# Two heads side by side in the rows of TensorE, in units of 512 columns, and the causal cut of P moved to GpSimd

## The chip, the cores and the metric

One core of one Trainium2 chip runs the whole program in one launch. The metric is the device time in microseconds (us); before the change three runs gave a median of 1901.57 us (1899.66 to 1901.57).

## The reference

The input x has 2 batches of 1024 tokens of width 128. Three layers follow each other; the first and the third are the same function (here called the FFN layer):

```python
q, k, v = to_heads(split(x @ w_qkv, 3))                      # 16 heads of width 8
scores = einsum('bhqd,bhkd->bhqk', q, k) / sqrt(8)
attn = softmax(where(causal, scores, -big))
o = einsum('bhqk,bhkd->bhqd', attn, v) -> (b, s, 128) @ w_o
h = layernorm(x + o); then a mixture of 8 experts (top 2, hidden width 512), layernorm
x = x + 0.5 * that
```

The middle layer is another attention, with selected keys. The change touches only the causal attention of 16 heads in the first and the third layer.

## The kernel before, in words

Every engine runs one hand-written instruction stream, and semaphores order them. One FFN layer is: layer norm (DVE), transposes and the products with w_qkv (PE), then the attention, then the output product, the gate and the 8 experts.

Attention goes in steps. A step is a pair of heads (`s` = 0, 1) of one batch; there are `PAIRS` = 16 steps per layer and 32 in the program. Since a head has only 8 dimensions, q and k are split into three bf16 parts each, and all nine products are stacked in the contraction: 72 rows (`ROWS`) of `QB[buf][s]` and `KB[buf][s]`, which SyncE's queue fills from DRAM (`sp_rows`, 12 loads of 24 rows and one of V a step; a ring of 4 buffers). The parts are made by a ping-pong between ScalarE (`p1_done`, `p2_done`) and VectorE (`r1_done`, `p3_done`) and spilled to DRAM first.

A step has two passes over the lower triangle of the 1024 x 1024 scores, each in 24 units of one head, one tile and at most 512 columns:

- Pass 1 (`pe_pass1`): scores with queries in partitions. PE adds the causal mask of a diagonal block with a product of the identity and `mask_qk`; VectorE takes the row maximum from PSUM (`dve_max`, line 1299). It runs one step ahead. `dve_maxrows` makes three bf16 parts of minus the maximum, PE transposes them (`pe_maxrows`, line 658), and ScalarE copies them as rows 96 to 98 into `QB` (`act_maxrows`, line 1065).
- Pass 2 (`pe_scores`): scores with keys in partitions, less the maximum (99 rows), again with a mask product (`mask_kq`, line 673). ScalarE takes the exponential from PSUM into `PT` (`act_exps`, line 1059).
- `pe_values` (line 687) multiplies V (32 columns: 8 of V, a 1 for the row sum, zeros) by P in float32. A float32 product is two passes over the array. Its output for head s and query half hf lies in strip (2s + hf) of 32 partitions of bank 6, so four strips can run side by side. It is called once for each key tile `kc`.
- ScalarE copies the result (line 1077), PE transposes it (line 696), VectorE divides by the sums and writes `ATT` (line 1328).

PSUM has three banks for pass 1, three for pass 2, one for the values, one for transposes. `pe_step` interleaves one unit of pass 2 with one of pass 1.

Of the kernel before, what the change touches and what calls it, by code (L numbers as in the profile page):

```python
# [16 lines left out]
P = 128  # L17
# [117 lines left out]
PT_RING = 8  # L135
# [12 lines left out]
def constants():  # L148

    f = np.float32  # L150
    q, k = np.arange(P)[:, None], np.arange(P)[None, :]
    sel = LW + np.arange(NSEL)[None, :]
    override = sel > q

    sign = np.where(np.arange(P) % DR < HALF, -1.0, 1.0)[:, None]
    c = {"ident": np.eye(P),
         "mask_qk": np.where(k > q, NEG, 0.0),
         "mask_kq": np.where(q > k, NEG, 0.0),
         "iota8": np.broadcast_to(np.arange(E), (P, E)),
         "nonlocal": np.where(k <= q, 3e38, -3e38),  # L160
         "keep": np.where(override, 0.0, 1.0),
         "fill": np.where(override, np.broadcast_to(sel, (P, NSEL)), 0.0),
         "key": np.arange(P)[:, None] + P * np.arange(4)[None, :],
         "swap": np.eye(P)[np.arange(P) ^ HALF],
         "sign": sign}
    return {n: np.ascontiguousarray(v.astype(f)) for n, v in c.items()}
# [33 lines left out]
def build(nc, ins, const_ap, rot_ap, mask_ap, out):  # L200
# [3 lines left out]
    q_rows = nc.dram_tensor("q_rows", (PAIRS, 2, HD, 3, L), BF16, kind="Internal").ap()  # L204
    k_rows = nc.dram_tensor("k_rows", (PAIRS, 2, HD, 3, L), BF16, kind="Internal").ap()
# [4 lines left out]
    with ExitStack() as ctx:  # L210
# [6 lines left out]
        bank = [ctx.enter_context(nc.psum_tensor(f"bank{i}", [P, BANK], F32)) for i in range(8)]  # L217
# [9 lines left out]
        mask_qk = sb("mask_qk_b", [P, P], BF16)  # L227
        mask_kq = sb("mask_kq_b", [P, P], BF16)
# [67 lines left out]
        qparts = view("ffn", (3, TOK), BF16)  # L296
        kparts = view("ffn", (3, TOK), BF16)
# [8 lines left out]
        rest = view("ffn", (2, BANK))  # L306
        VA = view("ffn", (PAIRS, 2, TB, STRIP))
        QB = [[view("ffn", (L,), BF16) for h in range(2)] for i in range(RING)]
        KB = [[view("ffn", (L,), BF16) for h in range(2)] for i in range(RING)]
        VS = [view("ffn", (2, TB, STRIP)) for i in range(RING)]  # L310
        OT = view("ffn", (BANK,))
        PT = [view("ffn", (BANK,)) for i in range(PT_RING)]
        rowmax = view("ffn", (2, 2, TB))
# [63 lines left out]
        qk_done, p1_done, r1_done, p2_done, p3_done = (sem(n) for n in ("qk_done", "p1_done", "r1_done", "p2_done", "p3_done"))  # L377
# [39 lines left out]
        EXP0, PV0, ATT0, GELU0, Y0, ACC0, MAX0, OTURN0, OT0 = S_RING, 2 * TB, 2, 4, 2, 2, S_RING, 1, 1  # L417
# [5 lines left out]
        def sp_rows(sp, c, it, buf):  # L423

            g = PAIRS * c
            if not isinstance(it, int) or c:
                sp.wait_ge(pv_done, PV0 + TB * (g + it - RING + 1))
            for s in range(2):
                for dst, src, axis in ((QB, q_rows, 1), (KB, k_rows, 0)):

                    rows = src[it:it + 1, s] if isinstance(it, int) else src[bass.ds(it, 1), s]
                    rows = rows.rearrange("a d r t -> r (a d) t").unsqueeze(axis).broadcast_to([3, 3, HD, L])
                    for i in range(3):
                        sp.dma_start(dst[buf][s][i * 3 * HD:(i + 1) * 3 * HD, :], rows[i]).then_inc(rows_loaded[buf], 16)
# [20 lines left out]
        def sp_ffn(sp, c):  # L455
# [118 lines left out]
        def pool_ffn(pool, c):  # L574
# [5 lines left out]
            pool_fill(pool, c)  # L580
            for n in (ln + 1, ln + 2):
                pool_rstd(pool, n)

        def pool_fill(pool, c):
# [5 lines left out]
            pool.memset(MB[:, :, :], 0.0)  # L590
            for buf in range(RING):
                for s in range(2):
                    pool.drain()
                    pool.memset(QB[buf][s][64:MAXROW, :], 0.0)
                    pool.memset(KB[buf][s][64:MAXROW, :], 0.0)
                    pool.drain()
                    pool.memset(KB[buf][s][MAXROW:MAXROW + MAXROWS, :], 1.0)
                pool.drain()
                pool.memset(spare[:, 3:4], float(c)).then_inc(filled, 1)

# [35 lines left out]
        def pe_pass1(pe, c, it, buf, u, visit):  # L636

            s, qt, hf = UNITS1[u]
# [3 lines left out]

            pe.wait_ge(max_done, MAX0 + N1 * n + u + 1 - S_RING)
            lo, hi = hf * BANK, min((qt + 1) * P, (hf + 1) * BANK)
            o = bank[u % S_RING]
            m = pe.matmul(o[:, 0:hi - lo], QB[buf][s][0:ROWS, qt * P:(qt + 1) * P], KB[buf][s][0:ROWS, lo:hi], start=True, stop=True)  # L646
            if hi == (qt + 1) * P:
                m = pe.matmul(o[:, hi - lo - P:hi - lo], ident_b[:, :], mask_qk[:, :], start=False, stop=True, skip_group_check=True)  # L648
            m.then_inc(s1_done, 1)

        def pe_maxrows(pe, c, it):
# [5 lines left out]
            for qt in range(TB):  # L657
                m = pe.transpose(mt[:, qt * P:(qt + 1) * P], MB[:, qt, :], ident_b[:, :])
            m.then_inc(mt_done, 1)

        def pe_scores(pe, c, it, buf, w):

            s, kc, hf = UNITS2[w]
            n = PAIRS * c + it
            if w == 0:
                pe.wait_ge(maxrow_ready, 2 * n + 2)

            pe.wait_ge(exp_done, EXP0 + N2 * n + w + 1 - S_RING)
            lo, hi = max(kc * P, hf * BANK), (hf + 1) * BANK
            o, rows = bank[S_RING + w % S_RING], MAXROW + MAXROWS  # L670
            m = pe.matmul(o[:, 0:hi - lo], KB[buf][s][0:rows, kc * P:(kc + 1) * P], QB[buf][s][0:rows, lo:hi], start=True, stop=True)  # L671
            if lo == kc * P:
                m = pe.matmul(o[:, 0:P], ident_b[:, :], mask_kq[:, :], start=False, stop=True, skip_group_check=True)  # L673
            m.then_inc(st_done, 1)

        def pe_values(pe, c, it, buf, kc):

            units = [w for w in range(N2) if UNITS2[w][1] == kc]
            n = PAIRS * c + it
            if kc == 0:  # L680
                pe.wait_ge(ot_ready, OT0 + n)
            pe.wait_ge(exp_done, EXP0 + N2 * n + units[-1] + 1)
            for w in units:
                s, _, hf = UNITS2[w]
                lo = max(kc * P, hf * BANK)
                r = (2 * s + hf) * STRIP
                m = pe.matmul(bank[6][r:r + STRIP, lo - hf * BANK:BANK], VS[buf][:, s, kc, :],  # L687
                              PT[w % PT_RING][:, 0:(hf + 1) * BANK - lo], start=(kc == 0), stop=True, skip_group_check=True)
# [10 lines left out]
        def ahead_units(left):  # L699

            return [(1, u) for u in range(EARLY, N1) if left >= 1] + [(2, u) for u in range(EARLY) if left >= 2]

        def pe_step(pe, c, b, it, buf, left, visit):

            todo = ahead_units(left)

            def ahead(n):
                for _ in range(min(n, len(todo))):
                    a, u = todo.pop(0)
                    pe_pass1(pe, c, it + a, (buf + a) % RING, u, visit + (buf + a) // RING)  # L710

            for kc in range(1, TB + 1):
                for w in [w for w in range(N2) if UNITS2[w][1] == kc]:
                    pe_scores(pe, c, it, buf, w)
                    ahead(1)
                if kc == MAX_AT and left >= 1:
                    pe_maxrows(pe, c, it + 1)
                pe_values(pe, c, it, buf, kc - 1)
            if left >= 1:
                pe_first_scores(pe, c, it + 1, (buf + 1) % RING, ahead)  # L720
            pe_outputs(pe, c, it)

        def pe_first_scores(pe, c, it, buf, ahead):
            for w in [w for w in range(N2) if UNITS2[w][1] == 0]:
                pe_scores(pe, c, it, buf, w)
                ahead(1)

        def pe_ffn(pe, c):
# [3 lines left out]
            for n in range(8):  # L732
                if n % 2 == 0:
                    pe.wait_ge(xt_ready, NG * n_turn + n // 2 + 1)
                if n >= 4:
                    pe.wait_ge(r1_done, 8 * c + n - 3)
                pe.matmul(bank[4 + n % 4][:, :], w_qkv[:, (n % 2) * D:(n % 2 + 1) * D],
                          XT[:, (n // 2) * BANK:(n // 2 + 1) * BANK], start=True, stop=True).then_inc(qk_done, 1)
# [7 lines left out]
            pe.wait_ge(r1_done, 8 * (c + 1))  # L746
            for u in range(N1):
                pe_pass1(pe, c, 0, 0, u, 0)
            pe_maxrows(pe, c, 0)
            todo = list(range(EARLY))  # L750

            def ahead(n):
                for _ in range(n * EARLY // 4):
                    pe_pass1(pe, c, 1, 1, todo.pop(0), 0)

            pe_first_scores(pe, c, 0, 0, ahead)
# [1050 lines left out]
```

## Time and profile before

| | |
|---|---|
| median of 3 runs | 1901.57 us |
| the profiled execution's own time | 1901.23 us |
| its span, first to last instruction | 1899.4 us |
| PE busy / VectorE / ScalarE / GpSimd | 86% / 69% / 58% / 18% |
| granted clock of TensorE, mean | 0.885 of 2.4 GHz |

### The profile page before, as it was taken

What the parts mean: (1) busy time and instruction counts of PE and PEld (TensorE: products, weight loads), DVE (VectorE), ACT (ScalarE), POOL (GpSimd) and SP (SyncE); (2) the same over time, 40 slices, a digit from 0 to 9 for tenths busy, and PEclk for the clock granted to TensorE, in tenths of its full rate; (3) what the DMA queues carried; (4) which work ended last, traced back from release to release, by engine and by line L of the source; (5) the groups of instructions that cost most, each with busy time, mean ns of one, the idle gap of its engine ahead of it and who ended that gap; (6) DMA issues with size and microseconds to landing.
All of it is one profiled execution on the core that took longest, in us unless ns stands there. A gap on an engine that the chain in (4) does not pass through costs nothing.

```text
span 1899.4 us, 34045 instructions
## 1 busy us (share of the span) xinstructions
PE 1626.6 (86%) x10724; PEld 954.2 (50%) x10724; DVE 1316.8 (69%) x3191; ACT 1110.8 (58%) x2328; POOL 336.6 (18%) x343
## 2 busy tenths in 40 slices
PE   3699999879995836599999999984799999879995
PEld 2244444357774412355555555663344444357774
DVE  5577777467778565777768787645677777557777
ACT  3276777558884534345446445542377677558873
POOL 6000000000001050154446444615000000000000
PEclk9599999969998755798689998996699999969998
DMA  4211111011110223411122121202111110011110
GB/s 139 72 43 49 46 47 35 1 57 67 66 56 16 81 67 83 92 56 32 52 65 72 36 57 55 77 24 94 68 48 45 53 44 31 1 57 67 66 56 23
DMA packets 67657, 104.28 MB, mean 55 GB/s; under 512 B 19560, under 2 KB 37424, under 8 KB 65456
## 3 DMA queue, kind: packets, MB, share of 16 engines
q1 hardware_dynamic: 57872, 84.87, 14.2%
q0 software_dynamic: 8192, 16.79, 3.3%
q8 instruction: 73, 1.20, 0.3%
q10 hardware_dynamic: 1456, 0.90, 0.2%
q14 instruction: 64, 0.52, 0.1%
HBM read 74.80 MB, written 8.59 MB: 44 GB/s over the span
## 4 chain that ended last, share of the span: by engine, by line
PE 71%; DVE 12%; ACT 5%; issue 4%; DVEq 4%; SPq 2%; DMA 1%; ACTq 0%; POOL 0%; POOLq 0%
PE bank L687 11%; PE bank L833 9%; PE bank L671 8%; PE bank L646 7%; PE bank L823 6%; PE bank L987 5%; PE bank L1000 2%; PE bank L1015 2%; PE bank L1003 2%; DVEq L1624 2%; PE bank L1031 2%; PE bank L968 2%; ACT experts L1132 2%; PE bank L648 2%; PE bank L673 2%
## 5 line engine op out<-in xcount | busy, mean ns | idle before, releaser
L1299 DVE TENSOR_REDUCE arena<-bank 128x1 f32<-128x512 f32 (+3 forms) x768 | 382.8, 551 | 168.9 <-PE bank L648 115.7
L1059 ACT ACTIVATE arena<-bank 128x512 f32<-128x512 f32 (+3 forms) x768 | 335.3, 493 | 143.8 <-PE bank L673 121.2
L624 POOL DMA_INDIRECT arena<-kv_rows,IDX x256 | 251.8, 984 | 368.3 <-PE bank L1034 244.1
L646 PE MATMUL bank<-arena 72*128 72x512 bf16 (+3 forms) x768 | 259.5, 346 | 38.9 <-DMA arena<-arena 36.9
L671 PE MATMUL bank<-arena 99*128 99x512 bf16 (+3 forms) x768 | 254.2, 335 | 6.1 <-ACT arena L1065 4.3
L572 POOL TENSOR_TENSOR rstd<-vareps,neghalf 128x8 f32<-128x8 f32 x14 | 23.2, 1659 | 1170.8 <-DVE vareps L1292 1170.8
L687 PE MATMUL bank<-arena 128*32 128x512 f32 (+3 forms) x1536 | 225.4, 501 | 0.0
L1357 DVE TENSOR_TENSOR experts<-arena,experts 128x512 fp32r<-128x512 f32 x256 | 171.5, 689 | 70.7 <-ACT experts L1132 70.7
L1130 ACT ACTIVATE arena<-bank,bias 128x512 f32<-128x512 f32 x256 | 185.9, 726 | 45.8 <-PE bank L823 45.8
L823 PE MATMUL bank<-experts,experts 128*128 128x512 f32 x768 | 196.7, 403 | 7.5 <-ACT experts L1132 5.4
L1132 ACT ACTIVATE experts<-bank,bias 128x512 fp32r<-128x512 f32 x256 | 187.2, 731 | 0.0
L833 PE MATMUL bank<-experts,experts 128*128 128x512 f32 x768 | 182.1, 389 | 0.0
L671 PEld LDWEIGHTS bank<-arena 99*128 99x128 bf16 x768 | 75.3, 98 | 204.1 <-ACT arena L1059 139.9
L823 PEld LDWEIGHTS bank<-experts,experts 128*128 128x128 f32 x768 | 143.6, 192 | 54.7 <-ACT experts L1132 22.3
L833 PEld LDWEIGHTS bank<-experts,experts 128*128 128x128 f32 x768 | 144.2, 188 | 30.4
L1264 ACT ACTIVATE ATT<-bank,col 128x256 f32<-128x256 f32 x128 | 60.7, 474 | 133.9 <-DVE col L1697 132.1
L1688 DVE TENSOR_TENSOR HN<-bank,RT 96x512 f32<-96x512 f32 x128 | 87.0, 680 | 71.2 <-PE bank L987 59.6
L646 PEld LDWEIGHTS bank<-arena 72*128 72x128 bf16 x768 | 77.8, 101 | 109.8 <-DVE arena L1299 44.5
L648 PE MATMUL bank<-mask_qk_b,ident_b 128*128 128x128 bf16 x512 | 117.2, 230 | 0.0
L673 PE MATMUL bank<-mask_kq_b,ident_b 128*128 128x128 bf16 x512 | 113.0, 222 | 0.0
L987 PE MATMUL bank<-XN,arena 128*96 128x512 bf16 x408 | 111.7, 416 | 0.2 <-DVE HN L1688 0.2
L1270 ACT ACTIVATE ATT<-ATT,inverse 128x256 f32<-128x256 f32 x128 | 64.6, 505 | 74.6 <-DVE inverse L1702 74.4
(249 smaller groups left out, 2436.4 us busy)
## 6 DMA issues: line engine op xcount, KB each, us to landing
arena<-wt_rows SPq DMA_DIRECT2D x16, 1024.0 KB, 4.9
arena<-q_rows SPq DMA_DIRECT2D x192, 48.0 KB
arena<-k_rows SPq DMA_DIRECT2D x192, 48.0 KB
arena<-in_L_ffn_w SPq DMA_DIRECT2D x32, 256.0 KB, 5.3
arena<-arena SPq DMA_DIRECT2D x32, 256.0 KB
XT<-idx_rows SPq DMA_DIRECT2D x16, 512.0 KB
arena<-kv_rows,IDX POOLq DMA_INDIRECT x256
arena<-HN SPq DMA_DIRECT2D x32, 128.0 KB, 2.4
```

Of the source, the lines that this page charges most:

```text
L624: pool.indirect_dma_start(G[d % GR][:, g, :], None, kv_rows, bass.IndirectOffsetOnAxis(ap=IDX[:, q, k * GB + g:k * GB + g + 1], axis=0))\
L646: m = pe.matmul(o[:, 0:hi - lo], QB[buf][s][0:ROWS, qt * P:(qt + 1) * P], KB[buf][s][0:ROWS, lo:hi], start=True, stop=True)
L671: m = pe.matmul(o[:, 0:hi - lo], KB[buf][s][0:rows, kc * P:(kc + 1) * P], QB[buf][s][0:rows, lo:hi], start=True, stop=True)
L687: m = pe.matmul(bank[6][r:r + STRIP, lo - hf * BANK:BANK], VS[buf][:, s, kc, :], PT[w % PT_RING][:, 0:(hf + 1) * BANK - lo], start=(kc == ...
L823: m = pe.matmul(bank[f][:, :], W1R[buf][w][:, f * P:(f + 1) * P], XR[x][:, tb * BANK:(tb + 1) * BANK], start=((w, x) == pairs[0]), stop=(( ...
L833: m = pe.matmul(bank[4 + k][:, :], W2R[buf][w][:, f, :], H1R[k][x][:, f, :], start=(f == 0 and (w, x) == pairs[0]), stop=(f == FC - 1 and ...
L987: m = pe.matmul(o[0:ROWKV, :], TAB[part][:, 4 * b + c, 0:ROWKV], OH[OH_AT[x][c] % OHR][:, :], start=(c == 0 and part == 0), stop=(c == n - ...
L1059: act.activation(PT[w % PT_RING][:, 0:m], bank[S_RING + w % S_RING][:, 0:m], ACT.Exp, scale=float(HD) ** -0.5)\
L1130: act.activation(H1[tb % 2][:, f, :], bank[f][:, :], ACT.Gelu_apprx_tanh, bias=bias1[buf][:, f:f + 1])
L1132: act.activation(H1R[tb % 2][0][:, f, :], bank[f][:, :], ACT.Gelu_apprx_tanh, bias=bias1[buf][:, f:f + 1]).then_inc(gelu_done, 1)
L1299: dve.tensor_reduce(rowmax[:, hf, s, qt:qt + 1], bank[u % S_RING][:, 0:n], AX_X, ALU.max).then_inc(max_done, 1)
L1357: dve.tensor_tensor(H1R[tb % 2][1][:, f, :], H1[tb % 2][:, f, :], H1R[tb % 2][0][:, f, :].bitcast(F32), ALU.subtract)\
```

## The change

- Two parts of float32r in place of three of bf16, so 4 products of 8 rows: 32 rows, and 3 rows for the maximum, which are zero in pass 1 (`zero_rows`, loaded by DMA) and hold the maximum in pass 2. `ROWS` is 35. Both heads of a step share one `QB[buf]` and one `KB[buf]`: head 0 in partitions 0 to 34, head 1 in 64 to 98 (`TILE` = 64), that is in two row halves of TensorE.
- A unit is now both heads by 512 columns: 9 units (`UNITS`) in place of 24 in each pass. Segments of several tiles are packed into one unit (`PASS1`, `PASS2`). It fills two PSUM banks, a `twin`, and one VectorE or ScalarE instruction reads all 1024 columns.
- The query tiles are ordered `QORDER` = 0,3,4,7 and 1,2,5,6, so that both strips of a head have the same number of blocks. Values run in 5 groups of units (`GROUPS`).
- Both passes share three twins (`S_RING` = 3) in turn. Pass 1 runs two steps ahead. Pass 2 has no mask product; GpSimd sets the upper triangle of P to zero in `PT` (`pool_cut`), and the values wait for that (`cut_done`). Pass 1 keeps its masks only in the last two units (4 diagonal blocks each, one 512-column product a head).
- The split of q and k is one ScalarE copy and one VectorE subtraction per 512 columns.
- Ahead of the first pass 1 of each layer PE runs 64 bf16 products of 128x128 by 512 columns into bank 7, whose result is not used.

The core of the diff:

```diff
-UNITS1 = [(s, t, hf) for t in range(TB) for s in range(2) for hf in range(2) if hf * BANK < (t + 1) * P]
-UNITS2 = [(s, kc, hf) for kc in range(TB) for hf in range(2) for s in range(2) if (hf + 1) * BANK > kc * P]
+PASS1 = [[(4, 0, 4)], [(5, 0, 4)], [(6, 0, 4)], [(7, 0, 4)], [(3, 0, 3), (1, 0, 1)], [(7, 4, 3), (5, 4, 1)], [(2, 0, 2), (6, 4, 2)],
+         [(t, t, 1) for t in MORDER[:4]], [(t, t, 1) for t in MORDER[4:]]]
+PASS2 = [[(0, 0)], [(1, 0)], [(1, 1)], [(0, 1), (0, 7)], [(0, 2), (0, 5)], [(1, 2), (1, 6)], [(0, 3), (0, 6)], [(1, 3), (1, 5)],
+         [(0, 4), (1, 4)]]
+GROUPS = [(0, 1), (2, 3), (4, 5), (6, 7), (8,)]
...
+        def pool_cut(pool, c, it, buf, u):
...
+            pool.wait_ge(exp_done, done)
+            p = PT[(UNITS * buf + u) % PT_RING]
+            for at in diagonals(u):
+                cut = p[:, :, at * P:(at + 1) * P]
+                m = pool.affine_select(out=cut, in_=cut, pattern=[[0, 2], [1, P]], compare_op=ALU.is_ge, fill=0.0, base=0, channel_multiplier=-1)
+            m.then_inc(cut_done, 1)
...
+            for j, (qt, k0, blocks) in enumerate(PASS1[u]):
+                for s in range(2):
+                    r = slice(TILE * s, TILE * s + ROWS)
+                    q = QPLACE[qt]
+                    m = pe.matmul(bank[2 * slot + s][:, at * P:(at + blocks) * P], QB[buf][r, q * P:(q + 1) * P],
+                                  KB[buf][r, k0 * P:(k0 + blocks) * P], start=(j == 0), stop=True, skip_group_check=True)
...
+        def pe_scores(pe, c, it, buf, u, left):
+            if left >= 2:
+                pe.wait_ge(max_done, MAX0 + TOTAL * c + m + UNITS + EARLY - 1)
...
+        def pe_next(pe, c, it, buf, m, u, visit):
+            pe.wait_ge(exp_done, EXP0 + TOTAL * c + m)
+            pe_pass1(pe, c, it, buf, u, visit, (2 * ((u + HALFWAY) % UNITS) + 1) % S_RING)
...
+            two, one = (buf + 2) % RING, (buf + 1) % RING
+            for u in range(HALFWAY, UNITS):
+                pe_scores(pe, c, it, buf, u, left)
+                if left >= 2:
+                    pe_next(pe, c, it + 2, two, UNITS * it + u, u - HALFWAY, visit + (buf + 2) // RING)
+                if u == HALFWAY:
+                    pe_values(pe, c, it, buf, 1)
+                if u == HALFWAY + 1 and left >= 1:
+                    pe_maxrows(pe, c, it + 1)
+                if u == HALFWAY + 2:
+                    pe_values(pe, c, it, buf, 2)
...
+            for u in range(HALFWAY):
+                pe_scores(pe, c, it + 1, one, u, left)
+                if left >= 2:
+                    pe_next(pe, c, it + 2, two, UNITS * (it + 1) + u, u + EARLY, visit + (buf + 2) // RING)
+                if u == 0:
+                    pe_values(pe, c, it, buf, 3)
+                if u == 1:
+                    pe_values(pe, c, it, buf, 4)
+                if u == 3:
+                    pe_values(pe, c, it + 1, one, 0)
+            pe_outputs(pe, c, it)
+
+        def pe_warm(pe):
+            for _ in range(WARM):
+                pe.matmul(bank[7][:, :], ident_b[:, :], mask_qk[:, :, :].rearrange("p a q -> p (a q)"), start=True, stop=True)
...
+            pe_warm(pe)
+            for x in range(UNITS + EARLY):
+                pe.wait_ge(max_done, MAX0 + TOTAL * c + x - S_RING + 1)
+                pe_pass1(pe, c, x // UNITS, x // UNITS, x % UNITS, 0, (2 * x + 2) % S_RING)
```

## Rows read from the trace of the kernel before

**Rows 1.** The page: busy time of each engine, and the granted clock in 40 slices.
```profile
PE 1626.6 (86%) x10724; PEld 954.2 (50%) x10724; DVE 1316.8 (69%) x3191; ACT 1110.8 (58%) x2328; POOL 336.6 (18%) x343
...
PEclk9599999969998755798689998996699999969998
```

**Rows 2.** Busy time by stretches: stretch, length, PE, PEld, DVE, ACT, POOL, clock, DMA.
```profile
42.50:87.00 44.50, 25.03 (x104) 10.51 (x105) 20.74 (x47) 7.36 (x12) 4.23 (x6) 0.50 0.30 106
87.00:368.00 281.00, 277.75 (x2138) 122.48 (x2136) 192.91 (x483) 200.80 (x420) 0.00 (x0) 1.00 0.11 37
...
700.00:840.00 140.00, 97.55 (x487) 47.22 (x486) 88.26 (x171) 61.01 (x118) 30.61 (x31) 0.73 0.34 79
840.00:1000.00 160.00, 154.15 (x1208) 93.72 (x1205) 113.20 (x289) 75.55 (x213) 72.38 (x76) 0.81 0.18 51
1000.00:1200.00 200.00, 190.99 (x1673) 117.44 (x1674) 160.20 (x410) 107.70 (x301) 103.40 (x106) 0.94 0.20 55
```

**Rows 3.** The chain that ended last, 250 to 300 us: start, length, what.
```profile
257.84 0.45 PE bank L658 x8
...
264.36 0.44 PE bank L696 x4
...
275.85 0.45 PE bank L658 x8
```

**Rows 4.** Groups by line and shape, 120 to 330 us: count, busy, mean ns, idle before.
```profile
L1299 DVE TENSOR_REDUCE arena<-bank 128x1 f32<-128x512 f32 x140 | 91.9, 685 | 26.5 <-PE bank L646 19.1 <-PE bank L648 7.4
...
L1065 ACT ACTIVATE arena<-bank 3x1024 bf16<-3x1024 bf16 x22 | 22.3, 1013 | 1.7
...
L1299 DVE TENSOR_REDUCE arena<-bank 128x1 f32<-128x128 f32 x46 | 12.0, 282 | 0.0
```

**Rows 5.** PE's timeline, 196 to 199 us.
```profile
196.73 0.22 PE L648 MATMUL bank<-mask_qk_b,ident_b 128*128 128x128 bf16 x1
196.88 1.06 PE L687 MATMUL bank<-arena 128*32 128x384 f32 x8
197.88 0.23 PE L671 MATMUL bank<-arena 99*128 99x128 bf16 x1
```

**Rows 6.** Timelines of VectorE and ScalarE, 198 to 202 us: start, length, engine, line.
```profile
198.42 2.48 DVE L1299 TENSOR_REDUCE arena<-bank 128x1 f32<-128x512 f32 x4 [0.49 <-PE bank L646]
...
200.99 0.17 DVE L1307 TENSOR_TENSOR arena<-arena 128x8 f32<-128x8 f32 x1
...
202.05 0.23 DVE L1317 TENSOR_TENSOR arena<-arena 128x16 bf16<-128x16 f32 x1
...
199.03 1.09 ACT L1059 ACTIVATE arena<-bank 128x512 f32<-128x512 f32 x2 [0.22 <-PE bank L671]
```

**Rows 7.** The timeline at 640 us: two products of 64 rows.
```profile
640.87 0.30 PEld L968 LDWEIGHTS bank<-arena 64*128 64x128 f32 x4
640.88 1.13 PE L968 MATMUL bank<-arena 64*128 64x512 f32 x4
```

**Rows 8.** Groups on PE, 480 to 520 us, at full clock.
```profile
L833 PE MATMUL bank<-experts,experts 128*128 128x512 f32 x74 | 17.8, 389 | 0.0
```

**Rows 9.** The page and the groups on GpSimd.
```profile
L572 POOL TENSOR_TENSOR rstd<-vareps,neghalf 128x8 f32<-128x8 f32 x14 | 23.2, 1659 | 1170.8 <-DVE vareps L1292 1170.8
...
L611 POOL CAST maskb<-arena 128x1280 bf16<-128x1280 f32 x1 | 1.4, 1358 | 0.1
```

**Rows 10.** The timeline around the first attention stage.
```profile
39.64 2.80 ACT L1099 ACTIVATE arena<-bank 128x128 f32<-128x128 f32 x16
...
52.56 0.59 SPq L437 DMA_DIRECT2D arena<-arena  x1
...
57.08 0.26 PE L646 MATMUL bank<-arena 72*128 72x128 bf16 x1 [18.78 <-DMA arena<-arena]
...
367.55 0.35 DVE L1328 TENSOR_TENSOR ATT<-bank,arena 128x64 f32<-128x64 f32 x2
```

**Rows 11.** Busy time in a stretch of small products in the middle layer.
```profile
912.00:964.00 52.00, 50.14 (x317) 30.42 (x314) 33.33 (x84) 19.25 (x58) 22.78 (x24) 0.54 0.12 31
```

More of the change, by code:

```diff
@@ L674, in pe_scores @@
-            m.then_inc(st_done, 1)
-        def pe_values(pe, c, it, buf, kc):
-            units = [w for w in range(N2) if UNITS2[w][1] == kc]
+            if left >= 2:
+                pe.wait_ge(max_done, MAX0 + TOTAL * c + m + UNITS + EARLY - 1)
+            else:
+                pe.wait_ge(max_done, MAX0 + TOTAL * c + min(m + UNITS + EARLY - 1, TOTAL))
+                pe.wait_ge(exp_done, EXP0 + TOTAL * c + m - S_RING + 1)
+            slot = 2 * u % S_RING
+            for j, (g, kc, p, at) in enumerate(places(u)):
+                for s in range(2):
+                    r = slice(TILE * s, TILE * s + ROWS)
+                    x = pe.matmul(bank[2 * slot + s][:, at * P:(at + 4 - p) * P], KB[buf][r, kc * P:(kc + 1) * P],
+                                  QB[buf][r, (4 * g + p) * P:(4 * g + 4) * P], start=(j == 0), stop=True, skip_group_check=True)
@@ L679, in pe_values @@
+            x.then_inc(st_done, 1)
+        def pe_next(pe, c, it, buf, m, u, visit):
+            pe.wait_ge(exp_done, EXP0 + TOTAL * c + m)
+            pe_pass1(pe, c, it, buf, u, visit, (2 * ((u + HALFWAY) % UNITS) + 1) % S_RING)
+        def pe_values(pe, c, it, buf, group):
             n = PAIRS * c + it
-            if kc == 0:
+            if group == 0:
                 pe.wait_ge(ot_ready, OT0 + n)
[L682 to L688, printed above, removed]
+                pe.wait_ge(exp_done, EXP0 + UNITS * n + 2)
+            pe.wait_ge(cut_done, len(CUT) * n + len([u for u in CUT if u <= GROUPS[group][-1]]))
+            for u in GROUPS[group]:
+                for g, kc, p, at in places(u):
+                    for s in range(2):
+                        r = (2 * s + g) * STRIP
+                        m = pe.matmul(bank[6][r:r + STRIP, p * P:], VS[buf][:, s, kc, :],
+                                      PT[(UNITS * buf + u) % PT_RING][:, s, at * P:(at + 4 - p) * P], start=(kc == 0), stop=True,
+                                      skip_group_check=True)
@@ L1068, in act_step @@
         def act_step(act, c, b, it, buf, left, visit):
-            act_exps(act, c, it, range(1, MAX_AT + 1))
+            n = PAIRS * c + it
+            one = (buf + 1) % RING
+            for u in range(HALFWAY, UNITS):
+                act_exp(act, c, it, buf, u)
+                if left >= 1 and u - HALFWAY - 1 in (0, 1):
+                    act_maxrow(act, c, it + 1, one, u - HALFWAY - 1)
             if left >= 1:
-                act_maxrows(act, c, it + 1, (buf + 1) % RING)
-            act_exps(act, c, it, range(MAX_AT + 1, TB))
@@ L1074, in act_step @@
-            n = PAIRS * c + it
-            act.wait_ge(pv_done, PV0 + TB * (n + 1))
+                for u in range(2):
+                    act_exp(act, c, it + 1, one, u)
+            act.wait_ge(pv_done, PV0 + len(GROUPS) * (n + 1))
             act.wait_ge(o_turned, OTURN0 + n)
@@ L1078, in act_step @@
             if left >= 1:
-                act_exps(act, c, it + 1, (0,))
+                for u in range(2, HALFWAY):
+                    act_exp(act, c, it + 1, one, u)
         def act_ffn(act, c):
@@ L1100, in act_ffn @@
                 m.then_inc(va_ready, 1)
-            act_maxrows(act, c, 0, 0)
-            act_exps(act, c, 0, (0,))
+            for s in range(2):
+                act_maxrow(act, c, 0, 0, s)
+            for u in range(HALFWAY):
+                act_exp(act, c, 0, 0, u)
             run_steps(act, act_step, c)
```

317 lines of the change are left out of this document (166 added, 151 removed).

## The prediction

> **What bounds the kernel now.** The page first [rows 1]: PE is busy 86% of the span, VectorE 69%, ScalarE 58%. Then the stretches [rows 2]: in the attention stage (87 to 368 us) PE is busy 277.75 of 281 us at the full clock of 2.4 GHz, VectorE 192.91, ScalarE 200.80. Then the chain [rows 3]: the same event of two successive steps lies 275.85 - 257.84 = 18.01 us apart, with PE in the chain all along. So a step costs PE 18.0 us, and 32 steps are 576 of the 1899 us. The rest of the time is not changed. The stage as a whole runs from the first pass 1 at 57.1 us to the last write of ATT at 367.9 us [rows 10]: 310.8 us, of which the first 30 are at half clock (42.5 to 87 us: 0.50) [rows 2]. The third layer shows the same pattern of clock (slices 28 to 34, [rows 1]), so every term below counts twice.
>
> **PE in a step after the change.** A unit's two products go to two row halves. The only such pair in the trace [rows 7]: four passes of 512 columns, 1.13 us in all. A float32 pass of 512 columns is 0.43 us at full clock (see the values), so four in a row would last 1.7 us: the halves ran side by side, and the loads of their weights too (four in 0.30 us, 0.11 for each further pair). A float32r product of 512 columns takes 17.8/74 = 0.24 us [rows 8]. A unit is 0.24 us then, 0.29 where it has a segment of one block, since 0.11 for its weights exceeds its columns, and 0.44 for the two pass 1 units of four such segments. Pass 1: 5 x 0.24 + 2 x 0.29 + 2 x 0.44 = 2.7; pass 2: 5 x 0.24 + 4 x 0.29 = 2.4. The masks of pass 1: 512 columns at 2.4 GHz are 0.22; 2 units x 2 x 0.22 = 0.9.
>
> Values: one call of four strips with 512 columns in the longest starts at 196.88 and the next product at 197.88 [rows 5]. That is 1.00 us: 0.85 of columns (two passes of 0.43), and 0.15 around them. So a block of 128 columns is 0.213, whatever the number of strips. Before, the longer strip has 26 blocks a step; the new order of query tiles gives 18 to each. 18 x 0.213 = 3.8, and 0.5 for turns between the segments of five calls: 4.3. Transposes of the maxima 0.45 and of the outputs 0.44 [rows 3]. Turning from one shape of the array to another costs 0.09: the mask product of 53 ns starts at 196.73, the values at 196.88 [rows 5]; 15 turns are 1.4. Sum 2.7 + 2.4 + 0.9 + 4.3 + 0.9 + 1.4 = 12.6 us in place of 18.0.
>
> **VectorE and ScalarE in a step.** Four reductions of 512 columns last 2.48 us, the last one 0.68, so their starts lie 0.60 apart [rows 4, 6]. 512 more columns at 1.05 ns (the slope from 282 to 685 ns, [rows 4]) make 1.13. Nine are 10.2; the maxima's chain (200.99 to 202.28, [rows 6]) with a first reduction that is new 1.4; the outputs 0.8: 12.4 us. Exponentials of 512 columns start 0.49 apart (1.09 - 0.60 for two, [rows 6]); 1024 make 0.92. Nine are 8.3, the copies of the maxima 2 x 1.04 [rows 4], the output 0.6: 11.0 us.
>
> **How they fit together.** All three engines now need nearly the same time, and only three twins stand between them. Unit m of pass 2 needs the maximum of the pass 1 unit two places earlier, and the next pass 1 unit needs the exponential before it. Laying the order of pe_step over the durations above, with 0.2 us from the end of a product's columns to its reader, PE stands: 1.4 us before unit 7 (the maximum of unit 0 is behind dve_outputs), 0.4 before the next step's unit 0 (row copies), 0.7 before pass 1 unit 4 and 0.8 before unit 7 (an exponential behind the output copy), 0.2 in small ones. 12.5 + 3.5 = 16.0 us a step at full clock: 2.0 saved, not the 5.5 that PE's sum shows.
>
> **The stage at full clock.** Ahead of the first output lie 13 pass 1 units at VectorE's 1.13 (15), the maxima and copies (4), five units of both kinds (8) and the rest of step 0 (15): 42 us. Then 13 steps of 16.0 and two without pass 1 of 9.5: 42 + 208 + 19 = 269 against 310.8.
>
> **Ahead of it.** The split loses its second round, so the copies of V, which start at 39.64 and last 2.80 [rows 10], end some 6.8 us earlier, at 35.6. The 64 products follow there, 64 x 0.216 = 13.8 us at full clock, to 49.4. The rows' loads take 11 issues in place of 13 (52.56 is the 13th, 4 us before PE's start [rows 10]), behind 4.2 MB of spilled rows in place of 3.1; I put them at 49. Both hide each other; pass 1 starts 7.6 us earlier. Without that cover (rows at 43) the 64 products would cost 6 us a stage.
>
> **GpSimd.** Eight cuts a step of 256 elements. The nearest rows: a cast of 1280 elements 1.36 us, a power of 8 elements 1.66 [rows 9]. Bounds 0.3 and 1.7 us. Values read a unit at least one exponential (1.5 us) later, so up to 1.7 the order of waits hides them; I take 0.6. Above 2.0 GpSimd itself would set the step (8 x 2.0 = 16).
>
> **The clock.** This is the term that decides. At half clock PE's streams double: 2 x 11.2 + 1.4 = 23.8 us a step. Before, PE had no gaps and kept 1.00. With gaps it didn't: 95% busy gave 0.94, 96% gave 0.81, 70% gave 0.73 [rows 2]. And a stretch of small products had 0.54 at 96% busy [rows 11], so busy time is not all. After the change PE stands 3.5 of 16 us, and its score products fill 70 of 128 rows. The first 13 units are worse: 0.24 of each 1.13 us. I take a clock of 0.90, between 0.81 and 0.94: a fifth of the time at half clock, 1/(0.8/16.0 + 0.2/23.8) = 17.1 us a step. The stage: 45 + 13 x 17.1 + 20 = 287. Saved: 310.8 - 287 + 7.6 = 31, twice 63 us. 1901.2 - 63 = 1838 us. The profiled execution (1901.23) is within 0.4 us of the median of the runs.
>
> The Trainium skill ("TensorE: Matmul & The Clock Gate", "A second HAM failure mode: psum-queue depth-cycling") speaks against the change: where a kernel cycles through PSUM banks, PE idles briefly between groups, and the clock goes back and forth. Three twins in turn are that case. By the page the first rival below would be the likeliest; no row of before has this pattern in the attention.
>
> **The rivals.**
> - The clock is mostly lost (0.25). For: [rows 11] and the gaps. Against: once up, it held 0.94 over 200 us of small products [rows 2]. The stage breaks even (318.4 with the earlier start) at (318.4 - 66)/13 = 19.4 us a step, which is a granted clock of 0.73, just that of 700 to 840 us. At 0.62: 1/(0.24/16.0 + 0.76/23.8) = 21.3, a stage of 50 + 277 + 22 = 349, 31 lost twice: 1963 us. All at half: near 2060.
> - The halves don't run side by side at one column a cycle (0.09); the pair of [rows 7] ran at half that rate. PE's sum grows by 5.1 to 17.7, its gaps close, 18.2 a step at full clock: 45 + 237 + 22 = 304, saved 14.4 twice: 1872 us.
> - The gaps are smaller than laid out (0.09): with VectorE as the bound (12.4) and 14.5 a step at full clock, 41 + 189 + 18 = 248, saved 70 twice: 1761 us.
> - The cuts last 2.3 us and GpSimd sets the step (0.04): 8 x 2.3 = 18.4, about 1885; slower only above 2.4.
> - The forecast, 0.53: 16.0 to 18.0 a step, so 1785 to 1885.
>
> **The numbers.** What differs by under 0.2% (3.8 us) from before, measurement can't tell. Faster: 0.53, with 0.09 and 0.09, less small shares of the rivals, 0.70. Same 0.04. Slower 0.26, nearly all the clock. The range reaches to the fast rival and to the nearer half of the lost clock: 1765 to 1955.
>
> **What would show it.** A step: the distance of L658's successor in the chain, 17.1 (16.0 if the clock is 1.00, 19.4 and more if I am wrong). PE busy in the stage by the profile falls from 99% to about 85 to 90%; the granted clock 0.90. L1299's successor 1.2 us a piece, spaced 1.13 at best, the exponential 1.02. GpSimd's cuts under 1.7 us and no long wait of the values for them. The first pass 1 near 49.5 us. It is wrong if the clock of the stage is below 0.75, or if value calls of segmented units last 1.5 us in place of 1.0 since strips wait for each other (four calls, 2 us a step, 18.0: 1885).

## The result, and the profile after

The changed kernel takes 2014.82 us (median of 4 runs, 2010.88 to 2017.99) against 1900.97 us for the kernel before beside it: a ratio of 1.061, 95% interval 1.059 to 1.063. It is 114 us slower, where the prediction had 1838 us and a range up to 1955. The span of the profiled execution grew from 1899.4 to 2009.1 us.

The page, with the lines that answer [rows 1]:

```profile
PE 1716.1 (85%) x10880; PEld 1061.9 (53%) x10916; DVE 1280.4 (64%) x2696; ACT 1056.6 (53%) x1832; POOL 411.1 (20%) x568
...
PEclk9656655678999765698889998977565655669998
```

PE has less to stream and is busy longer. The third to the eighth slice and the 30th to the 35th lie in the two attention stages: 9 in each of them before, 5 or 6 now. The stretches, as in [rows 2] (start and end, length, PE, PEld, DVE, ACT, POOL, clock, DMA):

```profile
57.40:87.00 29.60, 22.32 (x110) 12.62 (x112) 22.35 (x25) 7.08 (x7) 1.23 (x3) 0.50 0.17 69
87.00:368.00 281.00, 262.86 (x1750) 142.40 (x1758) 155.26 (x223) 143.66 (x149) 40.00 (x100) 0.59 0.10 36
245.00:368.00 123.00, 118.58 (x723) 64.28 (x726) 64.33 (x92) 59.72 (x62) 16.42 (x41) 0.50 0.09 34
...
1385.00:1757.00 372.00, 345.36 (x2240) 186.14 (x2254) 195.57 (x281) 184.87 (x192) 51.25 (x128) 0.56 0.09 32
```

In the stretch where PE had 1.00, it has 0.59, and from 245 to 368 us it stays at half clock (1.2 GHz) although it is busy 96% of the time. The chain in that part, as [rows 3] (start, length, what):

```profile
278.63 1.03 ACT arena L1145
...
281.79 1.86 PE twin L767 x8
...
288.31 1.86 PE twin L767 x8
...
293.55 1.88 PE twin L767 x16
...
302.87 1.03 ACT arena L1145
```

The same exponential comes back after 302.87 - 278.63 = 24.24 us, against 18.01 in [rows 3]. Nearly all of the chain is PE. PE's timeline gives the ends of both stages (the last transposes of outputs, L777) and the start of both:

```profile
57.40 1.65 PE L713 MATMUL twin<-ffn,ffn 35*128 35x512 f32 x6 [3.74 <-DMA arena<-arena]
...
420.31 0.63 PE L777 MATMUL twin<-const,arena 128*128 128x128 f32 x4 [0.81 <-ACT arena L1165]
...
1380.36 0.96 PE L713 MATMUL twin<-ffn,ffn 35*128 35x512 f32 x6 [3.92 <-DMA arena<-arena]
...
1757.61 0.63 PE L777 MATMUL twin<-const,arena 128*128 128x128 f32 x4 [0.81 <-ACT arena L1165]
```

Before, the trace has these four events at 57.08, 366.53, 1336.16 and 1644.53 us. So the first stage grew from 309.4 to 362.9 us (+53.5), the second from 308.4 to 377.2 (+68.9). The part between them shrank by 9.6, what follows by 3.4, and the start is 0.3 later: +109.7 us, the whole difference of the spans. The time is lost in the attention stages and nowhere else. Of the 9.6 us, 1.1 lie ahead of the third layer's stage and 8.5 in code that is the same in both kernels: from the last transposes of the first stage to the third layer's products with w_qkv (1305.57 us before, 1350.89 now) it is 939.0 us before and 930.6 now. This part differs from one profiled execution to the next, with 928.3 us in e4 below, which leaves it as it was before, and 925.5 in e2. The clock in it differs too: from 840 to 1000 us 0.81 before, 0.89 in e4.

### The profile page after: what moved, and what is told of

It is laid out like the page before. It is cut to its first block, busy times and chain, and to the rows that moved or that the text cites. A ratio compares the mean times of both kernels' runs of the same rounds, so it can differ in the third digit from the quotient of the medians.

```text
span 2009.1 us, 32622 instructions
## 1 busy us (share of the span) xinstructions
PE 1716.1 (85%) x10880; PEld 1061.9 (53%) x10916; DVE 1280.4 (64%) x2696; ACT 1056.6 (53%) x1832; POOL 411.1 (20%) x568
## 4 chain that ended last, share of the span: by engine, by line
PE 67%; DVE 12%; ACT 8%; issue 5%; DVEq 3%; DMA 2%; SPq 2%; ACTq 1%; POOL 0%; POOLq 0%
PE twin L767 11%; PE twin L924 9%; PE twin L747 7%; PE twin L713 6%; PE twin L914 6%; PE twin L1078 5%; ACT arena L1145 4%; PE twin L718 2%; PE twin L1091 2%; DVEq L1713 2%; PE twin L1106 2%; PE twin L1094 2%; ACT experts L1218 2%; PE twin L1122 2%; PE twin L1059 1%
## 5 line engine op out<-in xcount | busy, mean ns | idle before, releaser
L1145 ACT ACTIVATE arena<-twin 128x1024 f32<-128x1024 f32 x288 | 287.9, 1024 | 311.3 <-PE twin L747 308.0
L1398 DVE TENSOR_REDUCE arena<-twin 128x8 f32<-128x1024 f32 (+1 forms) x160 | 195.4, 1226 | 204.0 <-PE twin L718 129.1
L767 PE MATMUL twin<-arena 128*32 128x128 f32 (+3 forms) x1920 | 254.5, 653 | 2.1 <-POOL arena L658 1.5
L713 PE MATMUL twin<-ffn,ffn 35*128 35x128 f32 (+3 forms) x1152 | 202.9, 449 | 37.4 <-ACT arena L1145 21.0
L1389 DVE TENSOR_REDUCE arena<-twin 128x2 f32<-128x1024 f32 x128 | 154.6, 1223 | 125.0 <-PE twin L713 124.1
L1216 ACT ACTIVATE arena<-twin,bias 128x512 f32<-128x512 f32 x256 | 185.7, 725 | 46.0 <-PE twin L914 46.0
L747 PE MATMUL twin<-ffn,ffn 35*128 35x128 f32 (+3 forms) x960 | 197.4, 486 | 11.1 <-ACT ffn L1150 6.2
L914 PE MATMUL twin<-experts,experts 128*128 128x512 f32 x768 | 196.5, 403 | 7.6 <-ACT experts L1218 5.5
L1218 ACT ACTIVATE experts<-twin,bias 128x512 fp32r<-128x512 f32 x256 | 187.0, 730 | 0.0
L713 PEld LDWEIGHTS twin<-ffn,ffn 35*128 35x128 f32 x1152 | 143.4, 292 | 80.9 <-ACT arena L1145 49.9
L747 PEld LDWEIGHTS twin<-ffn,ffn 35*128 35x128 f32 x960 | 112.6, 275 | 134.5 <-issue 70.3
L924 PE MATMUL twin<-experts,experts 128*128 128x512 f32 x768 | 182.3, 390 | 0.0
L914 PEld LDWEIGHTS twin<-experts,experts 128*128 128x128 f32 x768 | 143.7, 192 | 54.7 <-ACT experts L1218 22.3
L924 PEld LDWEIGHTS twin<-experts,experts 128*128 128x128 f32 x768 | 144.2, 188 | 30.4
```

The source lines that it names most:

```text
L713: m = pe.matmul(bank[2 * slot + s][:, at * P:(at + blocks) * P], QB[buf][r, q * P:(q + 1) * P], KB[buf][r, k0 * P:(k0 + blocks) * P], star ...
L747: x = pe.matmul(bank[2 * slot + s][:, at * P:(at + 4 - p) * P], KB[buf][r, kc * P:(kc + 1) * P], QB[buf][r, (4 * g + p) * P:(4 * g + 4) * ...
L767: m = pe.matmul(bank[6][r:r + STRIP, p * P:], VS[buf][:, s, kc, :], PT[(UNITS * buf + u) % PT_RING][:, s, at * P:(at + 4 - p) * P], start= ...
L914: m = pe.matmul(bank[f][:, :], W1R[buf][w][:, f * P:(f + 1) * P], XR[x][:, tb * BANK:(tb + 1) * BANK], start=((w, x) == pairs[0]), stop=(( ...
L924: m = pe.matmul(bank[4 + k][:, :], W2R[buf][w][:, f, :], H1R[k][x][:, f, :], start=(f == 0 and (w, x) == pairs[0]), stop=(f == FC - 1 and ...
L1145: act.activation(PT[(UNITS * buf + u) % PT_RING].rearrange("p s n -> p (s n)"), twin[2 * u % S_RING][:, :], ACT.Exp, scale=float(HD) ** -0 ...
```

## The experiments

Ratios are to the kernel before on the same chip, whose median was 1896.56 us for the first four runs, 1898.82 for the next four and 1897.25 for the last four.

**Without the 64 products (e1).**

```diff
-WARM = 64
+WARM = 0
```

> The changed kernel without the 64 products ahead of pass 1 (nothing else changed). Clock theory: in the changed kernel the full clock that these products end with is gone at 57.3 us, as pass 1 begins, and the rows land only at 57.4 us, 3.7 us after the last of them. So they neither cost nor bring anything: about 2015 us, within 4 us of it, the first pass 1 again near 57 us. Rival (the 64 products carry some of the full clock into the stage, or draw the start out): a change of 10 us or more, up or down.

2024.39 us, ratio 1.067 (1.065 to 1.069). The first pass 1 starts at 58.4 us, so the start is the same within 1 us; the stage's clock is 0.57 in place of 0.59. In the medians it is 10 us slower than the change as it stands, and the intervals of the two ratios (1.067 here, 1.061 with the products) don't touch. So the clock theory's "within 4 us" missed, and the rival's 10 us or more came out. Whether the 64 products are worth that is not shown: the first pass 1 is 1 us later, and the unchanged part between the stages takes 936.9 us here against 930.6, a spread that it shows between other kernels too. They are not the loss.

**Rows of zeros up to 64 in each half (e2).** The padding is set once a layer by GpSimd.

```diff
-                    r = slice(TILE * s, TILE * s + ROWS)
+                    r = slice(TILE * s, TILE * s + TILE)          # in pe_pass1 and pe_scores
...
+                    pool.memset(QB[buf][TILE * s + PRODS:TILE * s + TILE, :].bitcast(F32), 0.0)
+                    pool.memset(KB[buf][TILE * s + PRODS:TILE * s + TILE, :].bitcast(F32), 0.0)
```

> The changed kernel with 29 more rows of zeros in each half, so that both score products contract over 64 rows in place of 35 and fill all 128 rows of TensorE (the result is the same, the columns streamed too). Theory A, the clock is lost since the score products leave 58 of 128 rows idle: the granted clock of the stage goes from 0.59 to 0.85 and more, a step from 22 to 24 us to 16 to 18 us, the kernel to 1840 to 1890 us. Theory B, the clock is lost to PE's short waits between units, whatever the rows: 0.59 stays, 2015 us within 10. Theory C, the steps are long for another reason than the clock (three twins, GpSimd's cuts): no change of the time even where the clock rises.

1835.67 us, ratio 0.969 (0.966 to 0.973): 179 us less than the changed kernel, with the same columns, the same order and semaphores, and 58 rows of zeros more in each pair of score products. That is Theory A, 4 us below its range. Page and stretches:

```profile
PE 1507.4 (82%) x10916; PEld 954.4 (52%) x10916; DVE 1281.8 (70%) x2696; ACT 1052.9 (57%) x1832; POOL 440.7 (24%) x600
...
PEclk9699999889997755799889998997799999879998
...
87.00:368.00 281.00, 228.99 (x2258) 131.33 (x2254) 198.04 (x334) 183.72 (x198) 53.61 (x127) 0.97 0.10 36
```

The clock of the stage is 0.97, although PE now waits more (busy 81%, before the padding 94%). This window reaches past the stage's end, which is at 342 us here; from 87 to 330 us the clock is 0.99 and PE busy 84%. A step is 16.5 to 16.8 us, but for two of the 13 full ones, of 18.4 and 17.8 us: from 147.7 to 166.1 us the clock is 0.91, from 216.3 to 234.1 us 0.90, and in the others 1.00. PE's timeline of one step (start, length, line, waits in brackets):

```profile
245.61 0.50 PE L751 MATMUL twin<-ffn,ffn 64*128 64x256 f32 x4
245.96 0.40 PE L717 MATMUL twin<-ffn,ffn 64*128 64x512 f32 x2
246.62 0.50 PE L751 MATMUL twin<-ffn,ffn 64*128 64x512 f32 x2 [0.27 <-ACT ffn L1154]
247.67 0.50 PE L717 MATMUL twin<-ffn,ffn 64*128 64x384 f32 x4 [0.55 <-ACT arena L1149]
248.10 1.08 PE L771 MATMUL twin<-arena 128*32 128x384 f32 x16
249.11 0.50 PE L751 MATMUL twin<-ffn,ffn 64*128 64x512 f32 x2
249.45 0.40 PE L717 MATMUL twin<-ffn,ffn 64*128 64x384 f32 x4
...
252.14 0.66 PE L717 MATMUL twin<-ffn,ffn 64*128 64x128 f32 x8 [0.46 <-ACT arena L1149]
...
259.29 0.62 PE L733 MATMUL twin<-ident_b,arena 128*128 128x128 bf16 x8 [0.68 <-DVE ATT L1431]
260.42 0.51 PE L751 MATMUL twin<-ffn,ffn 64*128 64x256 f32 x4 [0.51 <-DVE arena L1393]
```

These five waits are all that this step has: 0.27 + 0.55 + 0.46 + 0.68 + 0.51 = 2.47 us. Score units of one or two segments follow each other by 0.33 to 0.44 us (249.11, 249.45), those of four by 0.54 and more, and the value call of 16 products takes 249.11 - 248.10 = 1.01.

**A filler product in each unit (e3).** It goes into the unit's own bank, which the unit then overwrites.

```diff
+            pe_fill(pe, slot)          # ahead of the products of pe_pass1 and pe_scores
...
+            pe.matmul(bank[2 * slot][:, :], ident_b[:, :], mask_qk[:, :, :].rearrange("p a q -> p (a q)"), start=True, stop=True)
```

> The changed kernel with one more bf16 product of 128x128 by 512 columns ahead of each unit of both passes, into the unit's own bank, which the unit then overwrites: 18 a step, 0.22 us each at full clock (3.9 us a step), 0.43 at half (7.8). If the clock is the cause and dense products bring it back: granted clock of the stage 0.9 and more, a step of 16.0 + 2 to 3.9 = 18 to 20 us (part of it lies in PE's former waits), the kernel 1900 to 1960 us in spite of the added work. If the clock stays at half: 24.2 + 7.8 = 32 us a step and some 2260 us. If the waits on the three twins set the step and not the clock: about 24 us a step and more at full clock, 2015 us and more.

1956.97 us, ratio 1.032 (1.030 to 1.034): more work, and 58 us less than without it.

```profile
87.00:368.00 281.00, 280.65 (x2153) 131.59 (x2152) 168.74 (x244) 157.91 (x161) 43.43 (x108) 0.97 0.10 36
```

PE has no gap, the clock is 0.97 and a step 20.3 us. It is a second way to the clock, and a dearer one: a filler takes 0.31 us, 18 of them 5.6.

**The 64 products in the kernel before (e4).**

```diff
+            for _ in range(64):
+                pe.matmul(bank[7][:, :], ident_b[:, :], kparts[:, 0, 0:BANK], start=True, stop=True)
             for u in range(N1):
```

> One part of the change alone: the kernel before with 64 bf16 products of 128x128 by 512 columns ahead of its first pass 1 (moving data from the first part of k). Before, the stage's first 30 us (57 to 87 us) run at half clock, and PE is busy 99% after that. Theory, the dense stream of before holds a clock that it is given: these 30 us shrink to about 15, twice, 1901 - 30 = 1871 us, less what the products delay the start (13.8 us at full clock against a wait of about 12 for the rows, 27 us if they run at half). Rival, pass 1 loses the clock at once here as in the changed kernel: 1901 us or up to 10 more.

1891.54 us, ratio 0.999 (0.997 to 1.001): no difference, as the rival had it. Pass 1 starts at 57.8 us, the clock falls to half at 62.7 and comes back at 86.6 us. So the dense stream of before doesn't hold a clock that it is given either. In the 5 us at full clock VectorE paces PE, since its 24 maxima follow each other without a gap. In the kernel before, at half clock, the same 24 took 11.53 us, so the 5 us at full clock were worth 0.3 us. The two rows, with the products and before:

```profile
58.18 11.24 DVE L1301 TENSOR_REDUCE arena<-bank 128x1 f32<-128x128 f32 x24 [17.85 <-PE bank L648]
...
57.55 11.53 DVE L1299 TENSOR_REDUCE arena<-bank 128x1 f32<-128x128 f32 x24 [17.10 <-PE bank L648]
```

The first copy of outputs comes at 99.2 us, as before. What the half clock costs from 62.7 to 86.6 us no run here shows, as none had it at full clock there.

**Rows of zeros in pass 2 alone (e5).**

> The changed kernel with the rows of zeros in pass 2 alone: its products contract over 64 rows in each half, those of pass 1 over 35 as in the change. If the rows at work decide in degree (0.59 with none padded, 0.97 with both), the granted clock of the stage lies between, at some 0.75 to 0.9, and the kernel at 1870 to 1960 us. If only one of the passes mattered, it would come out at 1836 us (pass 2) or 2015 us (pass 1).

1846.09 us, ratio 0.973 (0.969 to 0.977), clock 0.95 from 87 to 368 us. The first expectation missed: it isn't in proportion. The second, that pass 2 alone matters, isn't told apart from it, since the interval overlaps that of all rows padded (0.966 to 0.973). With pass 2 padded at least most of the loss is gone. Pass 1 was never padded alone, so whether its rows matter at all, or whether padding any half of the products would do, stays open.

**The kernel before, contracted over 35 rows (e6).**

```diff
-            m = pe.matmul(o[:, 0:hi - lo], QB[buf][s][0:ROWS, qt * P:(qt + 1) * P], KB[buf][s][0:ROWS, lo:hi], start=True, stop=True)
+            m = pe.matmul(o[:, 0:hi - lo], QB[buf][s][0:35, qt * P:(qt + 1) * P], KB[buf][s][0:35, lo:hi], start=True, stop=True)
...
-            o, rows = bank[S_RING + w % S_RING], MAXROW + MAXROWS
+            o, rows = bank[S_RING + w % S_RING], 35
```

> The kernel before with its score products of both passes contracted over the first 35 rows alone (it had 72 and 99): columns, order and waits are those of before, PE is as busy as before, and part of the sum and the subtracted maximum are left out. Theory A, rows at work keep the clock: the stage loses the full clock, PE at half clock needs about 30 us a step in place of 18.0, a kernel of 2150 to 2280 us; with a clock that comes and goes 2000 or more. Theory B, only gaps of PE lose the clock: 1.00 stays, 18.0 us a step, 1897 us within 6.

2513.95 us in one run, further than expected.

```profile
87.00:368.00 281.00, 281.00 (x1028) 80.36 (x1027) 111.38 (x242) 105.59 (x200) 0.00 (x0) 0.54 0.07 22
```

PE is busy for all of the 281 us and has 0.54 of its clock; a step takes up to 39.9 us (232.3 to 272.2 us, all of it at half clock) in place of 18.0. Nothing of the change is in this kernel: no twin, no gap, no second head beside the first, no float32r. The only edit is to fewer rows, and the clock is lost with PE never waiting. That ends Theory B, in which only gaps lose it.

The edit has a second effect, which the expectation of 30 us a step left out: 39.9 is more than twice 18.0. At half clock in the kernel before, a mask product starts 0.11 us behind a score product of 128 columns (57.24 and 57.35 us); here it starts 0.22 us behind (255.84 and 256.06 us). So turning between 35 and 128 rows costs more here than between 72 and 128. This run alone can't tell the rows from the turns as what loses the clock. The zeros do: they leave the shapes in halves and their turns as they are, and the clock comes back.

**The masks of pass 2 by TensorE again (e7)** (with all halves at 64 rows; `pool_cut` does nothing, the values wait for the exponentials).

```diff
+                if QORDER[4 * g + p] == kc:
+                    for s in range(2):
+                        x = pe.matmul(bank[2 * slot + s][:, at * P:(at + 1) * P], mask_qk[:, 0, :], ident_b[:, :], start=False, stop=True,
+                                      skip_group_check=True)
```

> All halves at 64 rows as in the run before, and one part of the change undone: the mask of pass 2 is added by TensorE (16 bf16 products of 128 columns a step, by the identity) and GpSimd cuts nothing; the values wait for the exponentials alone. PE gets 16 x 0.06 = 1.0 us more a step. Theory (the cuts are hidden, PE's time is not): 16.7 becomes 17.2 to 17.7, about 1850 to 1865 us against 1836. Rival (the cuts hold the values up): no longer than 16.7, 1836 us or less.

1845.58 us, ratio 0.974 (0.971 to 0.977): 10 us slower in the medians than with GpSimd's cuts, which the overlapping intervals (0.966 to 0.973 there) don't tell apart, and less than the 14 or more expected. That part of the 1.0 us falls into PE's waits is likely but not shown. That the cuts hold next to nothing up is shown by the trace of the padded kernel that has them: from 100 to 330 us PE waits 0.8 us for GpSimd, in two places.

**64 rows, without the 64 products (e8).**

> All halves at 64 rows, and no 64 products ahead of pass 1. The full clock that they leave was gone at 55.95 us with the padding too, before the first pass 1 at 57.0, and it came back at 86.7 us. So they are worth nothing here either: 1836 us within 6. Rival: without them the clock comes back later, a few us more a layer, 1842 to 1850 us.

1840.81 us, ratio 0.971 (0.968 to 0.974), not told apart from 0.969. The clock comes back at 87.6 us, with them at 86.7.

**The outputs earlier in the step (e9)** (with 64 rows).

```diff
             for u in range(HALFWAY):
                 pe_scores(pe, c, it + 1, one, u, left)
+                if u == 3:
+                    pe_outputs(pe, c, it)
...
-            pe_outputs(pe, c, it)
...
-            dve_outputs(dve, c, b, it)
...
+            for u in range(UNITS):
+                dve_max(dve, c, it + 2, u)
+                if u == EARLY + 2:
+                    dve_outputs(dve, c, b, it)
+            dve_maxrows(dve, c, it + 2)
```

> All halves at 64 rows (step of 16.5 to 16.8 us at full clock, of which PE waits 2.5), and the outputs of a step (the 4 transposes of PE and VectorE's division) moved from the end of the step to between the scores of unit 3 and the next pass 1, on VectorE from behind the maxima's chain to between the 7th and the 8th maximum, where VectorE waits 0.9 us for PE. Theory (the outputs stand in the chain from maximum to scores, as the prediction's gap of 1.4 us had it): the waits of the transposes of the maxima (0.68 us) and of the first two score units after them (0.5) go in part, 15.5 to 16.0 us a step, 1810 to 1822 us against 1836. Rival (the three twins or ScalarE hold the step at the same length): 1836 us within 5.

1818.83 us, ratio 0.960 (0.958 to 0.962): 17 us less than with the padding alone. It has the lowest median of the twelve runs and beats both kernels. The same copy of outputs in two successive steps, and the stretch:

```profile
242.04 0.59 ACT L1170 ACTIVATE arena<-twin 128x512 f32<-128x512 f32 x1
258.18 0.59 ACT L1170 ACTIVATE arena<-twin 128x512 f32<-128x512 f32 x1
...
57.40:87.00 29.60, 21.70 (x114) 12.91 (x116) 22.02 (x24) 7.08 (x7) 1.23 (x3) 0.54 0.19 75
87.00:330.00 243.00, 209.38 (x2134) 115.50 (x2144) 177.76 (x261) 174.97 (x184) 49.92 (x124) 1.00 0.11 42
```

A step is 16.1 us. Not all of the gain is the wait: none of the 13 full steps is over 16.4 us, where the padded kernel had two of 18.4 and 17.8 at a lower clock, and these two make some 3 of the 10 us between the traces in 13 steps. PE's timeline shows where the rest of the wait went:

```profile
250.42 0.61 PE L733 MATMUL twin<-ident_b,arena 128*128 128x128 bf16 x8 [0.72 <-DVE arena L1421]
251.42 0.51 PE L751 MATMUL twin<-ffn,ffn 64*128 64x256 f32 x4 [0.39 <-DVE arena L1394]
...
259.21 0.66 PE L781 MATMUL twin<-const,arena 128*128 128x128 f32 x4
259.80 0.66 PE L717 MATMUL twin<-ffn,ffn 64*128 64x128 f32 x8
```

The transposes of the outputs fill the wait ahead of unit 7 of pass 1 (0.46 us, now none). The transposes of the maxima still wait 0.72 us, for VectorE's last part of the maximum (L1421) in place of the outputs: the chain was the maxima's as well.

**The second batch spilled behind the first rows (e10)** (64 rows), and **both moves**, with (e11) and without (e12) the 64 products.

```diff
+            spill(0)
...
             for k in range(RING):
                 sp.wait_ge(filled, RING * c + k + 1)
                 sp_rows(sp, c, k, k)
+                if k == 0:
+                    spill(1)
```

> All halves at 64 rows, and the spill of the second batch (2.1 MB) issued behind the loads of the first step's rows in place of ahead of them. Theory (the rows land at 57.4 us since they queue behind that spill): they land at 50 to 54 us, the first pass 1 starts at 53.3 us, right behind the 64 products, 3.7 us earlier in each layer: 1828 us. Rival (the rows' own small packets set the landing): 57 us and 1836 us as before.

1841.40 us, ratio 0.970 (0.969 to 0.972): no gain. The first rows land 1.6 us earlier, not the 3.7 expected, and the second step's later:

```profile
55.37 0.96 PE L720 MATMUL twin<-ffn,ffn 64*128 64x512 f32 x6 [1.10 <-DMA arena<-arena]
...
71.28 1.65 PE L720 MATMUL twin<-ffn,ffn 64*128 64x512 f32 x6 [5.40 <-DMA arena<-arena]
```

With the spill ahead these were 57.00 and 68.22 us. What the spill gave to step 0 it took from step 1, whose pass 1 stands in the stage's first part too.

> Both moves together, with all halves at 64 rows: if they add up 1803 to 1814 us.

1823.00 us, ratio 0.961 (0.960 to 0.963), not told apart from the early outputs alone (0.958 to 0.962): they don't add up, since the late spill brings nothing.

> The same without the 64 products. If the rows land before these products end (53.2 us), pass 1 starts earlier still, at 50 to 52 us, and the first units are paced by VectorE's maxima, not by PE's clock: 1 to 3 us less a layer than with them. Rival (their full clock is worth something once pass 1 follows without a pause): 3 us or more slower than with them.

1825.10 us, ratio 0.962 (0.960 to 0.964), not told apart from the run with them. Pass 1 starts at 55.7 us in place of 54.7, so the rows, not the 64 products, set the start.

## Why the prediction was wrong

The step that failed is **the clock**: "I take a clock of 0.90, between 0.81 and 0.94". It was 0.59 and 0.56. What happened is its own first rival (0.25), in a harder form than the one it worked out: 2014.82 lies between that rival's 1963 (clock 0.62, a stage of 349) and its 2060 (all at half). With the measured 24.24 us for a step at half clock and 16.6 at full (e2), 0.59 means 18% of the time at full clock: 1/(0.18/16.6 + 0.82/24.24) = 22.4 us a step, and the trace has 22.7 over the first stage's 13 full steps. The size of the loss follows from the clock within 0.3 us a step.

Why the clock failed: the prediction named two suspects, PE's waits and "its score products fill 70 of 128 rows", and priced the first by stretches of before (0.81 to 0.94) while it gave the second no price. The runs say it is the second. With all 128 rows and more waiting the clock was 0.97 (e2), without waits and with 35 rows 0.54 (e6), with dense products between the thin ones 0.97 (e3). What exactly the chip measures no run here shows; only that the same instructions over more rows, of zeros, change it, and that padding pass 2 alone is nearly enough. How many rows are enough was not tried either. [Rows 11] had a sign that busy time is not the measure, though no run shows why the clock was low there: 96% busy at 0.54. The prediction read it as "busy time is not all" and set the 0.94 of another stretch against it.

The Trainium skill's rule that the prediction cited ("TensorE: Matmul & The Clock Gate", "A second HAM failure mode: psum-queue depth-cycling") pointed to the right outcome by a mechanism that the runs don't bear out as the cause: three twins in turn with 2.5 us of waits a step keep 0.97, and two steps of 13 dip to 0.9. The Trainium skill's section "What's actually happening" ("TensorE: Matmul & The Clock Gate") has the clock set by how busy PE has been. By the busy time of the profile the stretch above, 96% busy at half clock, disagrees, so for this kernel that time is not the measure.

The other steps, one by one:

- **PE in a step**, 12.6 us: measured in e2 at full clock, by distances of starts less the waits, values 4.6 (4.3), pass 1 and pass 2 together 7.3 (2.7 + 2.4 and the 1.4 for turns: 6.5), masks 1.0 (0.9), transposes 1.2 (0.9): 14.0. A unit is 0.33 to 0.44 us where 0.24 or 0.29 was put; that the difference is the turn of 0.09, counted 15 times where nearly each of the 18 units pays it, is likely but was not tried.
- **The waits**, 3.5 us: 2.5. So 16.0 became 16.5 to 16.8: two errors of opposite sign. The wait by the outputs behind the maxima was where the prediction had it, 0.68 + 0.51 = 1.2 us against 1.4, the first part of it already ahead of the transposes; moving them gave 17 us (e9).
- **Row halves side by side**: yes, at one column a cycle, also at half clock. Value calls of segmented units take 1.0 us, as forecast.
- **VectorE 1.13 a unit, exponential 0.92 or 1.02**: 1.22 busy with starts 1.13 apart (three in 3.48 us), and 1.02.
- **At half clock 23.8 us**: 24.24.
- **The start**, 7.6 us earlier: 0.3 us later. The copies of V ended 2.9 us earlier, not 6.8, and the rows landed 9 us after their last issue. The 64 products were over 3.7 us before the rows and hid in that wait: they cost nothing, as forecast. Without them the changed kernel is 10 us slower (e1), which may or may not be theirs; with the rows padded the 5 us between the medians are not told apart from nothing (e8).
- **GpSimd**, 0.6 us a cut (0.3 to 1.7): 0.41 by the row below. Hidden, but for 0.8 us in 230 (e7). The row of the page:

```profile
L658 POOL TENSOR_SCALAR_AFFINE_SELECT arena<-arena 128x256 f32<-128x256 f32 x256 | 102.5, 406 | 675.9 <-ACT arena L1145 675.9
```

- **The sum at a full clock**: with the padding the kernel takes 1836 us where the forecast had 1838 for a clock of 0.90, but at 0.97, so that the two agree is luck. The first stage is 285 us (57.00 to 342.06) against 287, by the errors above cancelling; the 7.6 us by which each layer was to start earlier became 0.1 in the first and 1.1 ahead of the third. In their place 13.5 of the 66 us saved lie in the unchanged part between the stages (925.5 against 939.0 us), where the forecast had nothing and executions differ by that much anyway.

## What to carry to other kernels

Before shrinking a contraction on TensorE, ask what it does to the clock: here a product of few rows took the same columns, and the stage that such products fill ran mostly at half clock, though PE was busy. Padding with rows of zeros costs no column and gave back 9% of the whole kernel here. Read a row of the trace that contradicts your model (96% busy at 0.54) as a price to be paid, not as a caveat.

## What was not expected of the hardware

- PE busy 96% of 123 us stayed at half clock, and busy 100% of 281 us had 0.54 with 35-row products.
- Rows of zeros count: the clock went from 0.59 to 0.97 by padding 35 rows to 64 in each half, and to 0.95 by padding pass 2 alone.
- 64 dense bf16 products ahead of a stage didn't hold the full clock in it: in the changed kernel it was gone at 57.3 us, 3.7 us behind them and just ahead of the first pass 1; in the kernel before it lasted 5 us into pass 1, and the time stayed the same (0.999).
- A 128-column product starts 0.22 us behind one of 35 rows and 128 columns at half clock, and 0.11 us behind one of 72 rows.
